# A transformer layer on one core: the values weighed in three fp16 passes instead of one fp32 pass, with the splitting moved to VectorE and the attention steps set to other places

## What is computed

```python
h = einsum('bhid,oi,od->bho', x, weighted_sum, weight)          # token mixing
h = h + attention(layernorm(h))   # 16 heads of 16; q and k rotated and normed; softmax(q k^T / 4) v; out projection
h = h + ffn(layernorm(h))         # 8 experts: (relu(x W1 + b1)) W2 + b2, weighted by a thresholded sigmoid gate
```

## Time and profile before

| | |
|---|---|
| median of 3 runs | 1918.91 us (1918.88 to 1920.49) |
| profiled execution, time | 1918.81 us |
| its span, first to last instruction | 1917.0 us, granted TensorE clock 0.988 |
| PE busy | 1838.3 us, 96% |
| ACT, DVE, POOL busy | 1077.8, 698.6, 628.7 us |
| a steady iteration (six of them) | 227.7 to 229.7 us, PE busy 227.1 to 227.4 |
| first batch alone and its FFN, up to the first steady iteration | 374.1 us |
| last FFN | 170.9 us |

### The profile page before, as it was taken

How to read it: one execution, slowest core, us unless ns; L and a number is a source line. 1 busy time by engine, 2 the same in 40 slices (tenths; PEclk the granted TensorE clock), 3 DMA queues, 4 the chain that set the end, 5 groups by cost and what they waited for, 6 DMA issues and landing times.

```text
span 1917.0 us, 31838 instructions
## 1 busy us (share of the span) xinstructions
PE 1838.3 (96%) x12652; PEld 1168.6 (61%) x12652; DVE 698.6 (36%) x1575; ACT 1077.8 (56%) x1658; POOL 628.7 (33%) x537
## 2 busy tenths in 40 slices
PE   5679899999999999999999999999999999999999
PEld 4156545775467754677547764577546775466666
DVE  7867644554023621346103460144401453022001
ACT  3744676546655476545765457644665546654444
POOL 1012323334233342333323242333423334234443
PEclk9789999999999999999999999999999999999999
DMA  4322433415123151223313341232512315213221
GB/s 163 112 108 89 132 126 139 176 56 132 67 90 120 67 132 67 103 96 100 110 45 111 121 111 67 77 127 73 132 67 88 121 67 131 69 67 103 107 98 46
DMA packets 103971, 192.31 MB, mean 100 GB/s; under 512 B 67448, under 2 KB 80656, under 8 KB 87440
## 3 DMA queue, kind: packets, MB, share of 16 engines
q1 hardware_dynamic: 103824, 190.28, 30.7%
HBM read 153.55 MB, written 20.97 MB: 91 GB/s over the span
## 4 chain that ended last, share of the span: by engine, by line
PE 85%; DVE 3%; DMA 2%; ACT 2%; issue 2%; SPq 0%; DVEq 0%; ACTq 0%
PE bank_h L995 32%; PE bank_f L1014 11%; PE bank_f L1017 10%; PE bank_f L1016 10%; PE bank_o L903 6%; PE bank_s L889 4%; PE bank_s L801 3%; PE bank_s L802 3%; PE bank_s L803 3%; DMA kt<-stack 1%; DMA kt<-probs 1%; ACT hh L778 1%; PE bank_m L915 1%; PE bank_s L949 1%; PE bank_m L810 1%
## 5 line engine op out<-in xcount | busy, mean ns | idle before, releaser
L644 POOL TENSOR_TENSOR hl<-h,hh 128x512 f16<-128x512 f32 x512 | 602.9, 1178 | 1202.7 <-ACT hh L778 688.4
L995 PE MATMUL bank_h<-x,w1s 128*128 128x512 f16 x3072 | 750.0, 381 | 5.2 <-ACT hh L778 4.6
L775 ACT ACTIVATE h<-bank_h,b1s 128x512 f32<-128x512 f32 x512 | 351.3, 686 | 479.4 <-PE bank_h L995 479.2
L1014 PE MATMUL bank_f<-w2s,hh 128*128 128x256 f16 x2048 | 560.4, 274 | 2.3 <-DVE acc L1255 2.3
L1017 PE MATMUL bank_f<-w2s,hl 128*128 128x256 f16 x2048 | 558.8, 273 | 0.0
L1016 PE MATMUL bank_f<-w2s,hh 128*128 128x256 f16 x2048 | 558.8, 273 | 0.0
L995 PEld LDWEIGHTS bank_h<-x,w1s 128*128 128x128 f16 x3072 | 287.9, 99 | 331.0 <-issue 43.7
L778 ACT ACTIVATE hh<-bank_h,b1s 128x512 f16<-128x512 f32 x512 | 349.9, 683 | 0.0
L744 ACT ACTIVATE probs<-bank_s 128x1024 f32<-128x1024 f32 x240 | 246.3, 1026 | 161.5 <-PE bank_s L889 160.6
L1014 PEld LDWEIGHTS bank_f<-w2s,hh 128*128 128x128 f16 x2048 | 201.4, 98 | 107.1 <-issue 40.6
L1255 DVE SCALAR_TENSOR_TENSOR acc<-bank_f,gw,acc 128x256 f32<-128x256 f32 x256 | 106.1, 477 | 368.9 <-PE bank_f L1017 368.7
(11 more groups left out here) (187 smaller groups left out, 1451.5 us busy)
## 6 DMA issues: line engine op xcount, KB each, us to landing
w1s<-w_parts SPq DMA_DIRECT2D x56, 1024.0 KB, 4.8
w2s<-w_parts SPq DMA_DIRECT2D x56, 1024.0 KB, 4.8
raw<-in_w_dram SPq DMA_DIRECT2D x16, 1024.0 KB, 6.6
xraw<-in_x_t_dram SPq DMA_DIRECT2D x30, 512.0 KB, 4.8
w_parts<-w1s SPq DMA_DIRECT2D x8, 1024.0 KB, 8.7
w_parts<-w2s SPq DMA_DIRECT2D x8, 1024.0 KB, 10.9
out_dram<-acc SPq DMA_DIRECT2D x16, 256.0 KB, 6.1
w1s<-in_x_t_dram SPq DMA_DIRECT2D x2, 512.0 KB, 8.6
```

The lines of the kernel that those rows point to most:

```text
L644: pool.tensor_tensor(hl[n % HBUFS][:], h32[n % 2][:], hh[n % HBUFS][:], ALU.subtract)\
L775: act.activation(h32[n % 2][:], bank_h[n % 2][:, :], ACT.Relu, bias=b1s[:, e, m:m + 1]).then_inc(h_hi.sem, 1)
L995: last = pe.matmul(bank_h[n % 2][:, :], w[:, wp, k, m * P:(m + 1) * P], x16s[fb % 2][:, xp, k, :], start=(k == 0 and wp + xp == 0), stop=( ...
L1014: pe.matmul(o, high, w[:, 0, m, :], start=(m == 0 and t % 2 == 0), stop=False, skip_group_check=True)
```

## The change

- **Weighing in fp16.** For the six batches of the steady state (`ab >= 2`) the values are kept as two fp16 parts (`v16`), the exponentials as two (`halves`), and `weigh` is three passes of four matmuls: high by high, low by high, high by low. A scale, a power of two found from the weights' largest magnitudes, is put into the value weights and taken out of the output weights once, behind the second batch's attention (`scale_values`).
- **Who splits.** ACT writes the exponentials to one of three fp32 buffers (in `qk` and `stack`); a new step `halves` makes the two parts on VectorE, for each `scores` one copy and one subtraction of 128x1024. `weigh` waits for it. In `qkv` the values take three VectorE operations in place of one.
- **ReLU's low half** moves from POOL to VectorE, in all FFNs but the first, one chunk later in the list (`relu_low(n-1)` at `f1(n)`).
- **Places.** `mix` 1.6, 2.7, 3.8, 4.9; `ln1_turn` from 7.4, each 1.3; `qkv` 8.75 to 12.65; `qk_norm` 13.2; `unit` and `stack` 14.7 to 17.45; `scores` from 20.2, each 0.78; `weigh` one and a half such spaces later than before.
- **SP.** `turn_stacks` stands ahead of the load of expert 3.

The core of the diff:

```diff
-    steps += [(6.8, "ln1", 0), (15.7 - sooner, "qk_norm", 0), (24.0, "out_bias", 0)]
+    steps += [(mix[TT - 1] + 0.5, "ln1", 0), (norm, "qk_norm", 0), (20.0 if later else 24.0, "out_bias", 0)]
...
-    first = 25.6
+    first, pace, behind = (LATER_FIRST, LATER_PACE, 1.5) if later else (25.6, PACE, 0)
     for n in range(2 * UNITS):
-        steps.append((first + PACE * n, "scores", n))
+        steps.append((first + pace * n, "scores", n))
+        if later:
+            steps.append((first + pace * (n + 0.8), "halves", n))
     for u in range(UNITS):
-        steps.append((first + PACE * min(2 * u + 3, 2 * UNITS) + 1e-6, "weigh", u))
+        steps.append((first + pace * (min(2 * u + 3, 2 * UNITS) + behind) + 1e-6, "weigh", u))
...
+LATER_MIX = [1.6, 2.7, 3.8, 4.9]
+LATER_TURN, LATER_GAP, LATER_NORM = 7.4, 1.3, 13.2
+LATER_UNIT = [14.7, 15.55, 16.35, 17.15]
+LATER_FIRST, LATER_PACE = 20.2, 0.78
...
                 for e in range(2, EXPERTS):
-                    load_expert(b, e)
                     if more and e == 3:
                         turn_stacks(b + 1, range(TT))
+                    load_expert(b, e)
...
-                if stage == "f1":
+                if stage == "f1" and fb == 0:
                     wait(pool, h_hi, fb, 2 * (n + 1))
...
+                    if ab < 2:
+                        passes = [(v32[:, tile], probs[n % 2])]
+                    else:
+                        v_high, v_low = v16[:, 0, tile], v16[:, 1, tile]
+                        p_high, p_low = halves[n % 2][:, 0], halves[n % 2][:, 1]
+                        passes = [(v_high, p_high), (v_low, p_high), (v_high, p_low)]
+                    for k, (v, p) in enumerate(passes):
+                        for j in range(4):
+                            last = pe.matmul(bank_o[32 * j:32 * j + 32, :],
+                                             v[:, 4 * g + j].rearrange("p s d -> p (s d)"), p[:, j, :],
...
+            def relu_low(fb, n):
+                wait(dve, h_hi, fb, 2 * (n + 1))
+                wait(dve, f2_done, fb, n - HBUFS + 1)
+                dve.tensor_tensor(hl[n % HBUFS][:], h32[n % 2][:], hh[n % HBUFS][:], ALU.subtract)\
+                   .then_inc(h_lo.sem, 1)
...
+                if stage == "f1" and fb and n:
+                    relu_low(fb, n - 1)
...
+                    if ab >= 2:
+                        values = tmp_b[:, 0:D]
+                        wait(dve, summed, ab, n)
+                        half_v.link(dve, dve.tensor_tensor(values, at_v[:, 0:D], qkvb[:, 2 * D:QKV], ALU.add))
+                        values = values.rearrange("p (h d) -> p h d", d=HD)
+                        half_v.link(dve, dve.tensor_copy(v16[:, 0, n, :, 0, :], values))
+                        dve.tensor_tensor(v16[:, 1, n, :, 0, :], values, v16[:, 0, n, :, 0, :], ALU.subtract)\
+                           .then_inc(v_out.sem, 1)
...
+                elif stage == "halves":
+                    u, half = divmod(n, 2)
+                    high, low = (halves[u % 2][:, part, 2 * half:2 * half + 2, :] for part in range(2))
+                    wait(dve, weighed, ab, u - 1)
+                    wait(dve, exped, ab, n + 1)
+                    half_v.link(dve, dve.tensor_copy(high, exps[n % 3]))
+                    dve.tensor_tensor(low, exps[n % 3], high, ALU.subtract).then_inc(halved.sem, 1)
```

More of the change, by code:

```diff
@@ L62, in attention_order @@
     steps = []
-    mix, sooner, att_at = (FIRST_MIX, 1.5, FIRST_ATT) if first_ffn else (MIX, 0.0, range(TT))
+    later = not alone and not first_ffn
+    sooner, att_at = (1.5, FIRST_ATT) if first_ffn else (0.0, range(TT))
+    mix, unit = (FIRST_MIX, [u - 0.6 * sooner for u in UNIT]) if first_ffn else (LATER_MIX, LATER_UNIT)
+    turn, gap, norm = (LATER_TURN, LATER_GAP, LATER_NORM) if later else (9.0 - sooner, 1.5, 15.7 - sooner)
     for t in range(TT):
[L65 to L69, removed]
-    steps += [(6.8, "ln1", 0), (15.7 - sooner, "qk_norm", 0), (24.0, "out_bias", 0)]
+        steps += [(mix[t - 1] - 0.05 if t else 0.3, "split", t), (mix[t], "mix", t), (turn + gap * t, "ln1_turn", t),
+                  (turn + 0.05 + gap * (t + 1), "qkv", t), (turn + 0.1 + gap * (t + 1), "rotate", t),
+                  (unit[max(t - 1, 0)] + 0.1 * min(t, 1), "unit", t), (unit[t] + 0.3, "stack", t)]
+    steps += [(mix[TT - 1] + 0.5, "ln1", 0), (norm, "qk_norm", 0), (20.0 if later else 24.0, "out_bias", 0)]
     if alone:
@@ L140, in merge @@
         return order
-    between = {("scores", 0): [("maxima", 0), ("maxima", 1), ("reduce", 0), ("scales", 0),
+    between = {("scores", 0): [("v_max", 0), ("maxima", 0), ("maxima", 1), ("reduce", 0), ("scales", 0),
                                ("parts", 0), ("parts", 1), ("parts", 2), ("parts", 3)],
@@ L257, in build @@
         kt = sb("kt", [P, HEADS // 2, TOKENS], F16)
-        v1 = sb("v1", [P, TT, HEADS, 2, HD])
+        v16 = sb("v16", [P, 2, TT, HEADS, 2, HD], F16)
+        v32 = v16[:].rearrange("p a t h s d -> p (a t h s d)").bitcast(F32)\
+            .rearrange("p (t h s d) -> p t h s d", t=TT, h=HEADS, s=2)
         probs = [sb(f"probs{i}", [P, 4, TOKENS]) for i in range(2)]
+        halves = [p[:].rearrange("p j t -> p (j t)").bitcast(F16).rearrange("p (s j t) -> p s j t", s=2, j=4)
+                  for p in probs]
+        exps = [qk[:, 2 * i:2 * i + 2, :] for i in range(2)]
+        exps.append(stack[:].rearrange("p a h s d -> p (a h s d)").bitcast(F32).rearrange("p (j t) -> p j t", j=2))
         xh = sb("xh", [P, XK, P], F32R)
@@ L859, in steps @@
                         pe.wait_ge(set_lo, 3)
+                    if n == 0 and ab == 2:
+                        pe.wait_ge(v_scaled, 1)
                     high = [turned_h[:, n % 2, k, :] for k in range(DK)]
@@ L892, in steps @@
                     g, tile = divmod(n, TT)
-                    wait(pe, exped, ab, 2 * (n + 1))
+                    if ab < 2:
+                        wait(pe, exped, ab, 2 * (n + 1))
+                    else:
+                        wait(pe, halved, ab - 2, 2 * (n + 1))
+                    if n == 0 and ab == 2:
+                        pe.wait_ge(v_filled, 1)
                     if n == 0:
@@ L900, in steps @@
                         wait(pe, o_out, ab, g)
-                    for j in range(4):
-                        h = 4 * g + j
-                        last = pe.matmul(bank_o[32 * j:32 * j + 32, :],
-                                         v1[:, tile, h, :, :].rearrange("p s d -> p (s d)"),
-                                         probs[n % 2][:, j, :], start=(tile == 0), stop=(tile == TT - 1),
-                                         skip_group_check=True)
+                    if ab < 2:
+                        passes = [(v32[:, tile], probs[n % 2])]
+                    else:
+                        v_high, v_low = v16[:, 0, tile], v16[:, 1, tile]
[5 more added lines that the diff above has]
+                                             v[:, 4 * g + j].rearrange("p s d -> p (s d)"), p[:, j, :],
+                                             start=(tile == 0 and k == 0),
+                                             stop=(tile == TT - 1 and k == len(passes) - 1), skip_group_check=True)
                     last.then_inc(weighed.sem, 1)
@@ L963, in steps @@
                         wait(pe, o_out, 1, GROUPS)
-                    pe.matmul(sums_bank(n), v1[:, 0, 0, 1, 0:1].broadcast_to([P, P]), mx[:], start=True, stop=True,
+                    pe.matmul(sums_bank(n), v32[:, 0, 0, 1, 0:1].broadcast_to([P, P]), mx[:], start=True, stop=True,
                               skip_group_check=True).then_inc(maxima_summed, 1)
```

85 lines of the change are left out of this document (70 added, 15 removed).

## The result

The changed kernel takes 1962.14 us (median, 1960.58 to 1962.73) against 1918.95: a ratio of 1.0222, interval 1.0205 to 1.0238. It is slower by 43 us; the forecast was 1960. The profiled execution took 1960.58 us, with a span of 1958.8 against 1917.0.

A forecast was written before the change was run, and what follows sets the result against it. PE's own work bounds it (96% busy, at most 1.3 us of waiting to win). Per iteration -2.3 + 0.9 + 1.5 + 6.5 + 0.2 = 6.8; six make 40.8, plus 1 once, on 1918.8: 1960 us, range 1904 to 1984.

The forecast's parts named there:

- The chain from the fourth `qkv` to `scores` 0: Chain of 26.7 to 26.9 us against 19.5 of PE work: PE waits 7.4, before 0.87; +6.5 us an iteration.
- VectorE's load as a second proof: From `qkv` 0 to the end of `acc` 1, VectorE has 38 us of work where PE has 34; no gaps.
- `acc` 0: VectorE from `qkv` to `acc` 0: PE stalls 1.3 us at `f2`, 0.2 in `qkv` 2; +1.5 an iteration.
- The start: Start of an iteration: `mix` 0 waits 1.4 us for x's first low half, before 0.5; +0.9 us.
- PE's own work: Per iteration, fp16 weighing wins 3.2 us (0.80 against 1.00 each), mode changes 81 to 90 lose 0.9; net -2.3.
- The weights hide: In the weighing, loads of 0.08 us a set of four run under a 0.216 pass and cost nothing.
- the second rival: Weighing's weight loads do not hide: +0.24 x 96 = 23 us, 1983; chance 7%.
- The stretch of the scores: VectorE's 84 us, with 1.9 per `scores` for copy and subtraction, fit beside PE's 96; +0 to 2, taken as 0.2.
- The fourth rival: VectorE becomes the bound in the scores if the copy takes 1.22 us (99 against 96): 1975 to 1990; chance 13%.
- the third rival: Clock falls to 1.2 GHz behind one unbroken wait at `scores` 0: 1.7 us more an iteration, 1970; chance 15%.
- the likeliest case: Whole-kernel forecast at 43%: 1947 to 1975 us, with the chain's 6.5 between 5 and 8, the scores' 0.2 between 0 and 1.
- SP free of charge: On SP, expert 3's load waits until about chunk 19, needed at 24, over 10 us later: no cost.

The follow-up runs named there:

- e1: The changed kernel with the scores alone set later and closer (from 23.0, each 0.70, in place of 20.2 and 0.78): 1952.47 us.
- e2: The changed kernel with scores from 23.0, each 0.70, and unit and stack of tiles 2 and 3 set behind `acc` 1: 1927.95 us.
- e3: The changed kernel with `mix` 0 back at 2.1 (`mix` at 2.1, 2.8, 3.85, 4.9): 1960.97 us.
- e7: The changed kernel with each `weigh` 1.0 in place of 1.5 spaces later, right behind a `scores`: 1955.14 us.
- e6: The changed kernel without the weighing's pass of the low values, two passes in place of three: 1943.18 us.
- e4: The kernel before with one edit of the change alone, the stacks turned ahead of expert 3's load: 1983.65 us.
- e5: The changed kernel with relu's low half back on POOL in every FFN, all places as changed: 1968.92 us.

## Why the prediction was right, step by step

- **The chain from the fourth `qkv` to `scores` 0: right.** It named 26.7 to 26.9 us; the rows show 27.0. Of that, 12.1 lie ahead of the first transpose (predicted 8.7 + 2.7 = 11.4) and 14.9 behind it (15.3), with issues 11.3 apart from first to last and 3.3 a tile, as in the earlier trace rows. The waits were named in their places: `f1` 18 and 19 behind ACT, `f2` 16 behind `acc` 1, the rest at `scores` 0. By the brackets they are 5.2 to 6.6 an iteration, 5.9 in the mean, where the sum had 7.4. With the first 0.17 of each wait counted as waiting, the two iterations at the full clock wait 7.3 and 7.2. In the other four the clock fell in the middle of the stretch, and some 1.2 of waiting became slower work.
- **What the subtraction does not say.** Chain less work gives the wait as long as `scores` 0 stands at the end of the stretch. It does not say what would take the wait away: e1 put 28.2 us of work beside the chain and PE still idled 5.1, because each piece hangs on its own link (a stack's buffer, then the relu or `acc` behind it). e2, with the same work, moved those and idled 0.7.
- **VectorE's load as a second proof: wrong.** The load was right, 37.7 us busy against 38, but the text said that VectorE would have no gaps from `qkv` 0 to `acc` 1, and it has 4.6 us of them in the iteration shown: 0.2 to 0.8 at a time behind ACT's stacks, 1.07 behind ACT at an `ln1_turn`, the rest shorter. What holds it up at the stacks is the transposes, by way of the two stack buffers, and not its own work; e2 shows it, since there VectorE does the same work and PE's waits are gone.
- **`acc` 0: right.** Forecast 1.3 (its own times, 17.6 and 16.2, give 1.4) and 0.2, measured 1.23 and 0.1; a tile's stretch on VectorE was put at 4.5 and goes from 1123.29 to 1127.79.
- **The start: right.** 1.45 of wait against 1.4, `xl` 4.2 us into the iteration. But e3 shows that, with the chain as it was, this term was not additive: taking it away gave 0.2 us an iteration.
- **PE's own work: right in sign, the size off.** By the busy times it fell, in iterations with the full clock, from 227.2 to 225.7, by 1.5 and not 2.3. With the waiting that these count as work taken out, it fell by 3.0 (an estimate, as above). The term that was too small is the weighing, which takes 0.76 and not 0.80:

```profile
1190.18 0.39 PE L930 MATMUL bank_s<-qt,kt 64*128 64x512 f16 x2
1190.50 0.83 PE L955 MATMUL bank_o<-probs,v 128*32 128x512 f16 x12
1191.26 0.28 PE L1066 MATMUL bank_f<-w2s,hh 128*128 128x256 f16 x1
```

  That is 3.8 won in place of 3.2. The nine changes of mode at 0.1 each, 0.9, were right in count and price (the price as under e7): 3.8 less 0.9 is 2.9.
- **The weights hide: right.** e6's pass costs 0.20 and no more, so the second rival falls. The Trainium skill, TensorEngine Tiling (Gotcha 2: Feature Incompatibilities), says that column tiling rules out fast weight load. The trace does not speak against it: 32 columns of values, most of them fp16 now, load in 96 ns (the first row has min, median and max), about as long as the 108 of the fp32 ones in the earlier trace rows and as the 99 that 128 full columns take in `f1` (second row, mean):

```profile
L955 PEld LDWEIGHTS bank_o<-probs,v x1408: 92/96/153, 68.5 to 1729.7; 128*32 128x32 f16 x144, 128*32 128x32 f32 x32
...
L1047 PEld LDWEIGHTS bank_h<-x,w1s 128*128 128x128 f16 x3072 | 283.9, 99 | 321.2 <-issue 45.5
```

- **The stretch of the scores: right.** The copy of `halves` takes 0.69, between the two figures that the text had for it (0.59 and 0.747), the subtraction 1.23: 1.9, as put. The fourth rival needed a copy of 1.22. From `scores` 0 to the end of the last weighing it takes 96.0 to 96.6 us, with VectorE busy for 82.3 to 82.4; forecast were 96 and 84. The terms that the text lists for its 96 add up to 90.6, so that sum came out by an amount that it does not name.
- **The clock: the third rival came in part, elsewhere.** It falls at the wait for `acc` 1 in iterations 3 to 6, not at `scores` 0, and costs less than 1.7 there: 235.6 to 236.1 against 235.0, since the chain sets the end anyway. In e1, where it does not, an iteration with the fall is 2.1 longer than one without; its first two:

```profile
375.90:608.87 232.97, 224.92 (x1642) 144.41 (x1640) 168.03 (x313) 129.91 (x202) 3.34 (x1) 1.00 0.29 93
608.87:843.94 235.07, 226.79 (x1643) 144.99 (x1640) 168.09 (x313) 129.91 (x202) 3.34 (x1) 0.99 0.29 93
```

- **The sum: the waits right, the last tenth luck.** It came out at 6.8 an iteration, as forecast: by the busy times from +7.5 of waits (forecast +9.1) and -0.7 of work (-2.3), by the estimate of the first section from +8.9 and -2.1. The work at the full clock fell by 0.7 more than forecast, and the half clock, a rival that the sum had at nothing, gave 0.9 back. These two have nothing to do with each other, and that they cancel is luck. The lower end of the likeliest case, 1947, does not follow from the bounds beside it, which give 1950.
- **SP free of charge: right by its place alone.** The load of expert 3 is in time here; e2 and e4 price the same edit at 8 and 64 us in other places.

Left open: a chain with shorter or overlapped transposes was not tried, nor stacks 2 and 3 set later with the scores where the change has them.

## What to carry to other kernels

An order written by hand has a chain in it that is covered by exactly so much of the main engine's work; before moving its end forward, time the chain from the trace and count the work that is left beside it. More work beside the whole chain does not help a step that waits in the middle of it. When waits for three different engines appear in one stretch, look for the one buffer behind them: here two steps that waited for a stack to be emptied stood ahead of what PE needed, and setting them behind it gave back 24 us with nothing made faster. A step taken out of a queue's order is paid for by what it overtakes: ask when that is needed, at the places that the rest of the change gives it. And a new step can part two others that a rule of the list looks for side by side, as `halves` parts `f1` and `scores`.

## What was not expected of the hardware

- At the half clock the `f2` matmuls of 256 columns follow each other by 0.21 us (1157.89, 1158.10) in place of 0.11, for 3.41 us at a time, with a granted clock of 0.50, the level of 1.2 GHz. PE had waited 0.45, 1.7 and the better part of 2.8 us in the 9 us before. Iterations 1 and 2 have the same waits and no fall, so these alone do not decide it.
- VectorE's operations took longer where POOL worked beside them. Where POOL makes relu's low half (e5), a subtraction of 128x1024 on VectorE goes from 1226 to 1442 ns in the mean; POOL's own 1275 ns for that half compare with 1178 in the kernel before, where VectorE does less, and with 688 on VectorE.
- The transposes by DMA keep 3.3 us from one tile to the next with a weight load ahead of them and without one (the changed kernel and e4). It is their own latency: in all three traces one lands 3.2 us behind its issue in the median, and each waits for the one of the tile before. A few take up to 5 us, in all three.
